# Banded attention: the maximum, the exponential and the copy of the turned weights over 16 heads at once

## What is computed

```
x = x + attn_a(layernorm(x))           # stage "band": the only one touched
x = x + ffn(layernorm(x))
x = x + attn_b(layernorm(x))
x = x + ffn(layernorm(x))

def attn_a(x):                         # 16 heads of width 8
    q, k, v = heads(x @ WqT + bq) * 8**-0.5, heads(x @ WkT + bk), heads(x @ WvT + bv)
    scores = q @ k.T + mask            # mask: -1e30 outside chunk and left context
    return merge(softmax(scores) @ v) @ WoT + bo
```

## Time and profile before

| | us |
|---|---|
| median of three executions | 2094.34 |
| the profiled execution's own time | 2094.95 |
| its span in the trace | 2093.2 |
| the 36 tiles of the band stage, first score matmul to last reciprocal's input | 70.4 to 268.4 |

### The profile page before, as it was taken

How to read it: one execution, slowest core, us unless ns; L and a number is a source line. 1 busy time by engine, 2 the same in 40 slices (tenths; PEclk the granted TensorE clock), 3 DMA queues, 4 the chain that set the end, 5 groups by cost and what they waited for, 6 DMA issues and landing times. The chain is left out here.

```text
span 2093.2 us, 54880 instructions
## 1 busy us (share of the span) xinstructions
PE 1936.4 (93%) x21984; PEld 1288.2 (62%) x21984; DVE 1776.4 (85%) x2721; ACT 1239.3 (59%) x2204; POOL 1476.4 (71%) x1044
## 2 busy tenths in 40 slices
PE   1799979999938999999999999999999999899998
PEld 1466654444415777777777777777777777544444
DVE  5577768888677999999999999999999998787876
ACT  2445545666625666666666666666666665466665
POOL 3100005565647999999999999999999999155565
PEclk9999969999968999999999999999999999699999
DMA  4222237885410000000000000000000000477772
GB/s 126 80 74 77 70 86 125 148 137 119 65 32 11 17 10 17 10 15 11 13 14 13 13 13 13 11 16 9 13 6 9 6 10 2 83 133 154 143 128 57
DMA packets 95453, 109.20 MB, mean 52 GB/s; under 512 B 31712, under 2 KB 56672, under 8 KB 94816
## 3 DMA queue, kind: packets, MB, share of 16 engines
q1 hardware_dynamic: 92368, 103.91, 23.7%
q10 hardware_dynamic: 2832, 1.79, 0.3%
HBM read 88.10 MB, written 17.57 MB: 50 GB/s over the span
## 5 line engine op out<-in xcount | busy, mean ns | idle before, releaser
L938 DVE TENSOR_REDUCE head_shift<-head_score 128x64 bf16<-128x1024 f32 x512 | 624.1, 1219 | 84.7 <-PE head_score L750 72.9
L1133 POOL TENSOR_TENSOR ffn_sw<-ffn_sg,ffn_wide 128x512 f32<-128x512 f32 x256 | 325.0, 1270 | 491.6 <-ACT ffn_sg L1244 481.0
L900 ACT ACTIVATE head_ex<-head_score 128x1024 f32<-128x1024 f32 x512 | 524.7, 1025 | 187.9 <-PE head_score L772 186.2
L707 POOL TENSOR_TENSOR head_half<-head_ex 128x1024 f32<-128x1024 f32 x256 | 604.8, 2363 | 26.6 <-ACT head_ex L900 26.6
L945 DVE TENSOR_TENSOR head_ex<-head_ex,head_recp 128x1536 f32<-128x1536 f32 x256 | 446.6, 1745 | 6.2 <-ACT head_recp L872 6.2
L782 PE MATMUL head_den<-head_half,c_ident 128*128 128x128 f32 x3072 | 387.6, 276 | 2.9 <-POOL head_half L708 2.9
L782 PEld LDWEIGHTS head_den<-head_half,c_ident 128*128 128x128 f32 x3072 | 365.5, 193 | 6.6 <-POOL head_half L708 3.4
L714 POOL TENSOR_TENSOR head_ex<-head_ex,head_recip 128x512 f32<-128x512 f32 x256 | 328.9, 1285 | 17.2 <-ACT head_recip L874 10.1
L772 PE MATMUL head_score<-head_shift,c_identb 128*128 128x512 bf16 x1024 | 309.1, 383 | 18.3 <-DVE head_shift L938 12.2
L750 PE MATMUL head_score<-att_b_HB,att_b_GR 96*128 96x256 f16 x2048 | 310.3, 273 | 11.7 <-DMA att_b_HB<-b_queries 11.0
L765 PE MATMUL head_outp<-head_ex,att_b_vs 128*32 128x128 f32 x8192 | 277.9, 277 | 0.0
(11 more groups left out here) (236 smaller groups left out, 2547.2 us busy)
## 6 DMA issues: line engine op xcount, KB each, us to landing
ffn_wide<-pair_weights SPq DMA_DIRECT2D x256, 256.0 KB, 9.7
a_keys<-band_parts_k SPq DMA_DIRECT2D x14, 295.5 KB, 2.6
att_a_HB<-a_keys SPq DMA_DIRECT2D x56, 73.9 KB
a_queries<-band_parts_q SPq DMA_DIRECT2D x14, 271.5 KB, 3.0
att_a_GR<-a_queries SPq DMA_DIRECT2D x14, 271.5 KB
b_queries<-head_parts_q SPq DMA_DIRECT2D x32, 96.0 KB, 1.6
att_b_HB<-b_queries SPq DMA_DIRECT2D x128, 24.0 KB
b_keys<-head_parts_k SPq DMA_DIRECT2D x24, 96.0 KB, 1.6
```

What stands on the lines that cost most here:

```text
L707: ch.link(pool.tensor_tensor(hf, e[:, 0:8, :], e[:, 8:16, :], ALU.add))
L900: act.activation(ex[:, kt % RING, :, h * QS:(h + 1) * QS], score[:, h, :, :].rearrange("p k (a w) -> p (k a) w", a=NH // 2), ACT.Exp, scal ...
L938: dve.tensor_reduce(shift[:, h, :], score[:, h, :, :].rearrange("p k (a w) -> p w k a", a=NH // 2), AX.XY, ALU.max, negate=True).then_inc( ...
L1133: pool.tensor_tensor(sw[:, unit % 2, :], sg[:, unit % 2, :], wide[:, k % 2, i, :], ALU.mult).then_inc(sw_ready, 1)
```

## The change

The three semaphores of each step now count tiles and not halves. TensorE signals `score_ready` once, after both mask matmuls; VectorE takes the maxima of all 16 heads in one reduction of 1,024 columns; `take_maximum` waits for it once and signals `shifted` once, after its second matmul; ScalarE makes one exponential of 1,024 columns; `turn` waits for it, makes all eight transposes and signals once; ScalarE copies 1,024 columns at once; `attend` waits for that copy before its first matmul. The matmuls, their order and the work are the same. The other functions are not touched.

```
--- before.py
+++ after.py
@@ -381,7 +381,7 @@
                 tile, buf, col = b * NQT + t, t // GT, t % GT * QT
                 if t % GT == 0:
                     pe.wait_ge(placed, ONE + (b * NGRP + (t // GT + 1)) * (READS * 16))
-                pe.wait_ge(prob_ready, ONE + tile * 2)
+                pe.wait_ge(prob_ready, ONE + tile)
                 for g in range(NG):
                     for j in range(NSUB):
                         rows = slice(j * 32, j * 32 + 32)
@@ -392,29 +392,32 @@
                 for h in range(2):
                     rows = slice(0, P) if t in (0, NQT - 1) else slice(h * 32, h * 32 + 32)
                     lhsT = c["identb"] if t in (0, NQT - 1) else c["ident4"]
-                    pe.matmul(score[:, h, :].rearrange("p (a w) -> p a w", a=HH), lhsT[rows, :],
+                    last = pe.matmul(score[:, h, :].rearrange("p (a w) -> p a w", a=HH), lhsT[rows, :],
                               c["band"][rows, t, :][:, None, :].broadcast_to([rows.stop - rows.start, HH, KWIN]),
-                              start=False, stop=False, skip_group_check=True).then_inc(score_ready, 1)
+                              start=False, stop=False, skip_group_check=True)
+                    if h == 1:
+                        last.then_inc(score_ready, 1)
 
             def take_maximum(tile):
+                pe.wait_ge(shift_ready, ONE + tile + 1)
                 for h in range(2):
-                    pe.wait_ge(shift_ready, ONE + tile * 2 + (h + 1))
-                    pe.matmul(score[:, h, :].rearrange("p (a w) -> p a w", a=HH), c["identb"][:, :],
+                    last = pe.matmul(score[:, h, :].rearrange("p (a w) -> p a w", a=HH), c["identb"][:, :],
                               shift[:, h, :][:, :, None].broadcast_to([P, HH, KWIN]),
-                              start=False, stop=True, skip_group_check=True).then_inc(shifted, 1)
+                              start=False, stop=True, skip_group_check=True)
+                last.then_inc(shifted, 1)
 
             def turn(tile):
+                pe.wait_ge(probT_ready, ONE + tile)
+                pe.wait_ge(prob_ready, ONE + tile + 1)
                 for h in range(2):
-                    pe.wait_ge(probT_ready, ONE + tile * 2)
-                    pe.wait_ge(prob_ready, ONE + tile * 2 + (h + 1))
                     for j in range(GH):
                         last = pe.transpose(turned[:, h, j * P:(j + 1) * P], prob[:, h, j * P:(j + 1) * P], c["ident"][:, :])
-                    last.then_inc(turned_ready, 1)
+                last.then_inc(turned_ready, 1)
 
             def attend(tile, buf):
                 pe.wait_ge(attT_ready, ONE + tile)
+                pe.wait_ge(probT_ready, ONE + tile + 1)
                 for h in range(2):
-                    pe.wait_ge(probT_ready, ONE + tile * 2 + (h + 1))
                     for pp in range(2):
                         for g in (2 * h, 2 * h + 1):
                             pair = g % 2 * 2 + pp
@@ -484,12 +487,10 @@
             def batch(b, par):
                 for t in range(NQT):
                     tile = b * NQT + t
-                    for h in range(2):
-                        act.wait_ge(shifted, ONE + tile * 2 + (h + 1))
-                        act.activation(prob[:, h, :], score[:, h, :], ACT.Exp, scale=SCALE / ASCALE ** 2).then_inc(prob_ready, 1)
-                    for h in range(2):
-                        act.wait_ge(turned_ready, ONE + tile * 2 + (h + 1))
-                        act.activation(probT[:, h, :], turned[:, h, :], ACT.Copy).then_inc(probT_ready, 1)
+                    act.wait_ge(shifted, ONE + tile + 1)
+                    act.activation(prob[:, :, :], score[:, :, :], ACT.Exp, scale=SCALE / ASCALE ** 2).then_inc(prob_ready, 1)
+                    act.wait_ge(turned_ready, ONE + tile + 1)
+                    act.activation(probT[:, :, :], turned[:, :, :], ACT.Copy).then_inc(probT_ready, 1)
                     if t % GT < 2:
                         n = b * NGRP + (t // GT + 2)
                         if t % GT == 0:
@@ -554,10 +555,9 @@
             def batch(b, par, first):
                 for t in range(NQT):
                     tile = b * NQT + t
-                    for h in range(2):
-                        dve.wait_ge(score_ready, ONE + tile * 2 + (h + 1))
-                        dve.tensor_reduce(shift[:, h, :], score[:, h, :].rearrange("p (a w) -> p a w", a=HH),
-                                          AX.X, ALU.max, negate=True).then_inc(shift_ready, 1)
+                    dve.wait_ge(score_ready, ONE + tile + 1)
+                    dve.tensor_reduce(shift[:, :, :], score[:, :, :].rearrange("p h (a w) -> p h a w", a=HH),
+                                      AX.X, ALU.max, negate=True).then_inc(shift_ready, 1)
                     if t % GT > 0:
                         low_part(b * NGRP + (t // GT + 2), (par + t // GT) % 2, t % GT - 1, bank_q)
                     if not (first and t == 0):
```

## The result

| | us |
|---|---|
| before, median of six (three of them shown earlier) | 2092.92 (2091.74 to 2095.97) |
| after, median of six | 2101.34 (2100.27 to 2103.89) |
| ratio after to before | 1.0040, 95% interval 1.0027 to 1.0053 |
| difference of the medians | +8.4 |
| the profiled execution after: time, span | 2101.02, 2099.2 |

A forecast was written before the change was run, and what follows sets the result against it. TensorE, 94% busy in the band stage, was taken as the bound, so only its standstills count. Four sequences (6.7 us), first tile (0.5) and end (0.4) sum to +7.6 on 2094.34: 2102.0 us, range 2097 to 2108.

The forecast's parts named there:

- t = 2, 4, 5, 7: VectorE's chain shorter: In these tiles VectorE's chain gates; its reduction ends earlier and the output projection starts earlier, -0.07 us each.
- t = 3, 6: copy, then exponential: In these tiles the later copy delays `attend`, then the exponential ends later and holds the transposes, +0.43 us each.
- t = 1: maximum, then exponential: In this tile both matmuls wait for the whole reduction, then the transposes for the whole exponential, +0.57 us.
- t = 0: maximum, exponential: In this tile the reduction waits for both mask matmuls, so exponential and transposes come later, +0.39 us.
- t = 8: maximum over both mask matmuls: In this tile, gated by VectorE, the reduction waits for both mask matmuls: +0.21 - 0.07 = +0.14 us.
- first tiles, beyond these: The first tile's mask matmuls run at a lower clock, so it loses about 0.9 us, 0.5 more.
- end of the stage: At the band stage's end nothing hides the last, later copy; the reciprocal starts later, 0.4 us.
- The prices: One instruction of 1,024 columns takes 1.22 us (reduction) or 1.02 (exponential, copy), 0.07 less than its pair.
- Rival 1: Only the ends of the pairs count, from L402 to the transposes: not slower, 2092 to 2093 us; chance 0.06.
- Rival 2: TensorE's list absorbs the transposes' delay in t = 0, 3, 6: half the loss, 2097 to 2098 us; chance 0.15.
- Rival 3: A wide instruction costs as much as two end to end, 1.37 and 1.19 us: 2110 us; chance 0.05.
- Rival 4: Longer gaps lower TensorE's granted clock in the band stage, stretching tiles by tens of us; chance 0.02.

The follow-up runs named there:

- e1: Kernel before with only the copy of the turned weights made in one instruction, not halves; 2097.85 against 2093.32 us, ratio 1.0020.
- e2: Kernel before with only the exponential made in one instruction, not halves; 2095.91 us, ratio 1.0013.
- e3: Kernel before with only the maximum taken in one instruction, not halves; 2095.74 us, ratio 1.0011.
- e5: Kernel before, halves kept, with the reciprocal of the denominators moved from VectorE to ScalarE; 2082.68 against 2093.93 us, ratio 0.9944.
- e4: Kernel before with each step joined only in tiles where its later hand-over should be covered; 2092.47 against 2093.32 us, ratio 0.9996.
- e7: Kernel e4 with the reciprocal moved from VectorE to ScalarE; 2091.86 us, +9.2 us against e5.

## Why the prediction was right

The forecast was +7.6 us; the medians say +8.4 and the stage +8.6. That the median after, 2101.34, comes even closer to the 2102.0 forecast is chance, since the kernel before took 2092.92 in the later runs and not 2094.34. The mechanism is the one forecast, late hand-overs that cost where TensorE's list has no other wait, but the sum owes something to errors that cancel. Step by step, as the tiles show it:

| step | forecast | measured |
|---|---|---|
| t = 2, 4, 5, 7: VectorE's chain shorter | -0.07 | -0.06, -0.05 |
| t = 3, 6: copy, then exponential | +0.43 | +0.40 |
| t = 1: maximum, then exponential | +0.57 | +0.62 |
| t = 0: maximum, exponential | +0.39 | +0.24 |
| t = 8: maximum over both mask matmuls | +0.14 | +0.16 |
| first tiles, beyond these | 0.5 | 1.8 in the two profiles, 1.0 by the means |
| end of the stage | 0.4 | 0.7 |

The 36 tiles were put slightly too high (1.68 us a sequence against 1.60), the first tiles and the end together too low (0.9 against 1.7 to 2.5).

*The prices.* That one instruction of 1,024 columns saves 0.07 us and not a whole fixed cost held: 1.225 and 1.023 us against 1.29 and 1.09 for two. By the 125 ns that the Trainium skill (Perfetto Trace Analysis, Optimizing Scalar/DVE Operations) gives for a VectorE instruction on PSUM the gated tiles should have gained about twice as much; they gained 0.05 to 0.06, and the trace decides. That section's advice to break instructions up where an engine isn't saturated but causes bubbles on others agrees with e1, e2 and e3: each joined step costs 2.4 to 4.5 us, by idle time that it makes on TensorE.

*The late hand-overs.* Each was found where the forecast put it, the copy before L424 in t = 3 and 6 and the exponential before L414 in t = 1 by the profile's own naming, the exponential in t = 0, 3 and 6 by the 0.11 to 0.12 us from its end to the weight load. For t = 3 the forecast put this load at 4.16 us (189.34 less 185.18), 0.43 later than before; it came at 4.24, 0.52 later. The copy held the tile for longer than foreseen (the denominators start 0.39 or 0.40 later and not 0.33), and the load follows an exponential after 0.11 to 0.12 us and not after the 0.08 taken from the copy. The tile grew by only 0.40 because 0.11 of the 0.13 us in which `project` had waited for the addition was used up. So the +0.43 is close by luck: too small a delay, and an idle time overlooked. For t = 1, which has no such wait, the load came 0.62 later where 0.57 was foreseen, and the tile grew by 0.62.

*What was mis-sized.* The forecast says that the one wait of TensorE in t = 0, 1, 3 and 6 is 0.16 us for the maximum; the weight load of `project` also waited for the addition to `x`, 0.20 us in t = 0 and 0.13 in t = 3 and 6. For t = 0 the transposes' load was foreseen 0.39 later and came 0.43 later, but 0.19 of that fell into this wait, and the tile grew by 0.24. The same wait made e1's tiles 0.07 to 0.16 longer and e3's 0.08 longer than I expected, and kept e5's t = 4, 7 from losing what t = 2, 5 lost: one wait, overlooked in both directions. At the end of the stage I let the first denominator matmul start 0.08 us after the copy's end; the rows show 0.15, and the later start of the last tile's transposes (t = 8) belongs there too. In the first tile I scaled the loss with the clock and took the time of its return as given; it came at 79.5 and 79.4 us, 3.3 to 3.4 later than in the first profile of the kernel before, but only 1.5 to 1.6 later than in its second.

*Rival 1*, only the ends count, is refuted by e1 to e3. *Rival 2*, TensorE's list absorbs the exponential in t = 0, 3 and 6, fails for the change: these tiles grew by 0.24 and 0.40. It has a true part, as e2 shows: with the exponential alone joined, t = 1 pays its whole 0.46 but t = 0, 3 and 6 only 0.04 to 0.05; there the cost comes when the copy's delay, or in t = 0 the maximum's, is added. *Rival 3*, dearer wide steps, is refuted by their durations and by e4. *Rival 4*, a fallen clock, fails from the third tile on, where the granted clock is 1.00 (83 to 269 us). The first tiles run at the low clock in both kernels; whether the change makes it last longer there is not settled.

## What to carry to other kernels

Joining two halves saves the follower engine little when its two instructions already overlap (here 0.06 us of 1.29) and moves the first hand-over to the end of the second half (for the exponential from 0.60 to 1.02 us after its start, and the start itself comes later, since it waits for both halves). Before joining, list for each place of the leading engine's queue what it waits for last: where another engine's chain gates, joining is free; where nothing does, its whole delay counts; and the next kernel's improvement of that chain (here 9.7 us by the tiles and 11.3 by the medians for moving one reciprocal) takes the cover away, as -0.06 us turned into +0.20 to +0.35.

## What was not expected of the hardware

Two executions of one program whose tiles agree within 0.01 us from the tenth on differ by 2.6 to 3.1 us in attention b, at its start and after its last scores, where TensorE has gaps: behind the scores the granted clock is 0.78 or 0.89 in one execution and 1.00 in the other. Three of 13 profiles have the longer attention b. The eleven times of e7 fall into four at 2088.1 to 2089.4 and seven at 2091.3 to 2093.2 us; that the seven all had it, and the median is 3 to 4 us too high for the edit by this, is likely from the two that were profiled but not shown. A change worth under 3 us is better read from the tiles of a trace than from such times. In the same way the stretch of the low clock at the start of the band stage ended at 76.1 and 77.9 us in two profiles of the kernel before, and at 79.5 and 79.4 in two of the changed one.
